# DLRM tower on one core: the first chunk by blocks of 8 examples, one plan for the layer-0 products, the gathers in two halves of a chunk, and transposes from the common rows

## The chip, the cores and the metric

One NeuronCore of a Trainium2 chip. The metric is the time of one execution on the device in microseconds (us), lower is better; it is taken over several executions and the median counts.

## What is computed

For each of 512 examples, 39 rows of 16 numbers are looked up in 39 tables (1,000 to 125,000 rows each) by `ids`. On them run three layers of a compressed interaction network, then a small MLP:

```python
def _cin_layer(X0, Xi, W, b):                 # X0: (512, 39, 16)
    Wr = W.reshape(H, F0_, Fi)                # H = 128
    return jnp.einsum('hjk,bjd,bkd->bhd', Wr, X0, Xi) + b[None, :, None]
...
for W, b in Ws:                               # three layers, Fi = 39, 128, 128
    Xi = _cin_layer(X0, Xi, W, b)
    res.append(Xi.sum(axis=2))
...
h = jnp.concatenate([z, dense_ctx], axis=1)   # (512, 384 + 16)
h = jnp.maximum(h @ W_top1 + b_top1, 0.0)     # 512
h = jnp.maximum(h @ W_top2 + b_top2, 0.0)     # 256
y = h @ W_top3                                # (512, 1)
```

## The kernel before

The 512 x 16 columns (example, dimension) are cut into 16 chunks (n = 0 to 15) of 32 examples, 512 columns; a chunk has 4 blocks (i = 0 to 3) of 8 examples, 128 columns. All engines run one program each, in an order written out by hand; semaphores that only count up tie them together. In the code "at (i, g)" names a place in a chunk: block i, and behind it the group of PE (g, 0 to 9), of ACT (a, 0 to 5), of DVE (d, 0 to 3) or of GpSimd (k, 0 to 3) after which a step comes.

- GpSimd (POOL) gathers the table rows of a chunk with 10 indirect DMAs (`gather`, each 128 rows of 64 B) into `emb`, and between them adds staged parts for layer 1 (`add`, L227, four a block). In chunk n it gathers chunk n + 3, the ten at the places `GATHER_AT`. Chunks 0, 1 and 2 are gathered at the head.
- SP's queue runs strictly in order, and a wait in it holds all that stands behind: `write_x` (from `emb` to the scratch `x_rows` in HBM, two halves of two DMAs), `load_xrow` (2 DMAs, the 39 rows for the transposes), `load_x` (from the scratch, shifted copies `shifted` and three copies of the 39 rows, `rows3`: 9 DMAs, 1.9 MB), and `copy_diag` (8 DMAs a pair of blocks, `xt` into the block-diagonal `diag` that layer 2's matmul reads). `body(n, u)` of SP is: write_x of the second half of chunk n + 2, load_xrow(n + 2), load_x(n + 2), copy_diag(n, pair 1), write_x of the first half of chunk n + 3, copy_diag(n + 1, pair 0).
- ACT copies the common rows to PSUM (`store_rows`, L685), DVE multiplies them with the shifted rows (`multiply_l0`, L395, seven tiles a chunk), PE contracts the products (`layer0`, L495, fp32, two passes a tile) into `quad_ps`. ACT and DVE split the result into `x1_hi` and `x1_lo`.
- Layer 1 on PE (`layer1`, L525): for each block ten groups of four fields, each three matmuls of 512 columns (hi x hi, hi x lo, lo x hi). ACT scales six groups a block by `xt` (L697), POOL adds them up, DVE scales and adds the other four (L424) and reduces all to `x2t` (L436).
- Layer 2's first step, `g_block` (L555), multiplies `x2t` of block i with `diag` of that block: at (i + 1, 9), so the g block of (n, 2) follows the last group of chunk n. `layer1` carries its wait, on the second of its three matmuls:

```python
    multiply(x1_hi, w1_hi, start=True)
    if g_of:
        pe.wait_ge(diag_copied[g_of[1] // 2], 16 * BLK_B * (g_of[0] + 1))
    ...
    multiply(x1_hi, w1_lo)
```

- `layer2` (L568) runs three times: in chunk 8, in chunk 15 and at the end, where the MLP follows.

Weights of layer 1 (2.5 MB, three parts) come over ACT's queue at the head; all three are split into hi and lo before layer 1 starts. Chunks 2 to 7 and 10 to 13 are loops in the code, the others are written out.

Of the kernel before, what the change touches and what calls it, by code (L numbers as in the profile page):

```python
# [7 lines left out]
F32 = mybir.dt.float32  # L8
# [14 lines left out]
CW = 512  # L23
# [38 lines left out]
BUFS = 3  # L62
# [11 lines left out]
LATE_HIGH_X1_AT, LATE_LOW_X1_AT = (3, 2), (3, 2)  # L74
NEXT_PRODUCTS_AT = {(2, 2): 0, (2, 3): 1, (3, 2): 2, (3, 3): 3}
PRODUCTS_AT = {(0, 2): 4, (0, 3): 5, (1, 0): 6}
FIRST_PRODUCTS_AT = {(1, 1): 0, (1, 2): 1, (1, 3): 2, (2, 0): 3, (2, 2): 4, (2, 3): 5, (3, 0): 6}
SECOND_PRODUCTS_AT = {(0, 0): 0, (0, 2): 1, (0, 3): 2, (1, 0): 3, (1, 2): 4, (1, 3): 5, (2, 0): 6}
# [23 lines left out]
assert all(len(fields_of(g)) == GF for g in A_GROUPS) and DUP == FPG * HALF_G and W2_FIRST > 0  # L102


def build(nc, ids, bases, tables, x_rows, w0a, w0b, w1, w2, biases, b1_row, ctx_in, wt1, wt1c, bt1, wt2, bt2, wt3,
          ident_in, mask_in, out):
    with ExitStack() as stack:
# [31 lines left out]
        rows3 = sb("rows3", [PK, 2, CW])  # L139
# [4 lines left out]
        xrow = sb("xrow", [FIELDS, CW])  # L144
# [26 lines left out]
        rows_picked = sem("rows_picked")  # L171
# [25 lines left out]

        def gathers_until(m):

            return 16 * HALF_G * (1 if isinstance(m, int) and m < BUFS else m - (BUFS - 2))  # L200

        @block.gpsimd
        def _(pool):
            def pick_rows(m, buf):
                ids_now = ids_sb[:, bass.ds(m, 1), :].rearrange("p a g -> p (a g)")
                nc.gpsimd.tensor_tensor(rows_now[:, buf, :], ids_now, bases_sb[:, :], ALU.add
                                        ).then_inc(rows_picked, 1)

                pool.wait_ge(rows_picked, m + 1)
                nc.gpsimd.tensor_tensor(passed[:, :], bases_sb[:, 0:1], bases_sb[:, 0:1], ALU.add)  # L210

            def gather(buf, g):
                parts = 128 if g < GATHERS - 1 else LAST_G
                nc.gpsimd.indirect_dma_start(  # L214
                    out=emb[0:parts, buf, g, :], out_offset=None, in_=tables[:, :],
                    in_offset=bass.IndirectOffsetOnAxis(ap=rows_now[0:parts, buf, g:g + 1], axis=0),
                ).then_inc(gathered[g // HALF_G][buf], 16)
# [12 lines left out]
            def body(n, gathering=True):  # L230
                for i in range(BLKS):
                    for k in range(ADDS):
                        add(n, i, k)
                        step = GATHER_AT.get((i, k))
                        if gathering and step is not None:
                            if step in (0, HALF_G):
                                half = step // HALF_G

                                pool.wait_ge(written[half], 32 * (n + 3))
                                if half == 0:  # L240

                                    pool.wait_ge(gathered[1][BUFS - 1], gathers_until(n + 2))
                                    pick_rows(n + 3, BUFS - 1)
                                else:
                                    nc.gpsimd.tensor_tensor(passed[:, :], bases_sb[:, 0:1], bases_sb[:, 0:1],
                                                            ALU.add)
                            gather(BUFS - 1, step)

            pool.wait_ge(ids_loaded, 32)
            for m in range(BUFS):  # L250
                pick_rows(m, m)
                for g in range(GATHERS):
                    gather(m, g)
            body(0)
            with pool.Fori(1, CHUNKS - 3) as n:
                body(n)
            with pool.Fori(CHUNKS - 3, CHUNKS) as n:
                body(n, gathering=False)

        @block.sync  # L260
        def _(sp):
# [3 lines left out]
            def write_x(m, half, buf):  # L265
                there = value(gathers_until(m))
# [13 lines left out]
            def load_x(m, u):  # L280
                all_written = value(32 * (m + 1))
# [544 lines left out]
```

## Time and profile before

| what | value |
|---|---|
| median of 3 runs | 710.0 us (707.98 to 715.27) |
| the profiled execution, own time | 709.59 us |
| its span in the profile | 707.8 us |
| PE busy | 650.3 us, 92% |
| DVE, POOL, ACT busy | 506.6, 490.1, 479.0 us |
| mean granted clock of PE | 0.995 |

The span runs from the first to the last instruction; the own time has 1.8 us around it. A busy share of 92% does not say that PE works at its peak: its matmuls are pipelined and their ends modelled. Idle time before an instruction stands in brackets behind it with what ended it.

### The profile page before, as it was taken

Reading aid. Unit: us, or ns where it says so; the run is one execution under the profiler, and the core shown is the slowest. Engines: PE = TensorE matmul, PEld = TensorE weight load, DVE = VectorE, ACT = ScalarE, POOL = GpSimd, SP = SyncE. Lnnn points to the kernel's source line nnn. Section 1 sums busy time; section 2 is a strip of 40 time slices with the busy share of each in tenths; the row PEclk is TensorE's granted clock in tenths of the full one; section 3 lists DMA queues with packets and bytes.
Section 4 is the critical chain, followed back from the end, with each engine's and each line's share of the span. In section 5 each row is a group of like instructions: output and inputs, shape, how many; then the busy total and the mean of one; then the engine's idle time right before and its main releaser. Section 6 shows DMA issues by size and latency. Waiting matters only on the chain.

```text
span 707.8 us, 12139 instructions
## 1 busy us (share of the span) xinstructions
PE 650.3 (92%) x2622; PEld 469.6 (66%) x2622; DVE 506.6 (72%) x1177; ACT 479.0 (68%) x1730; POOL 490.1 (69%) x465
## 2 busy tenths in 40 slices
PE   0097889999999999999999999999989999999998
PEld 0055567777677777777787677777767777778763
DVE  2345588979697979798853797979777979784810
ACT  2145577878687878686935778787767868784802
POOL 5767478878787878888854787878786845453700
PEclk9999999999999999999999999999999999999999
DMA  8660425151515151515140041322323040002000
GB/s 208 126 131 12 110 38 114 40 109 27 120 29 118 28 119 28 120 28 118 29 109 13 10 113 17 81 49 67 63 61 67 7 116 4 2 4 81 0 1 0
DMA packets 65776, 44.51 MB, mean 63 GB/s; under 512 B 49563, under 2 KB 58062, under 8 KB 63860
## 3 DMA queue, kind: packets, MB, share of 16 engines
q1 hardware_dynamic: 54610, 39.35, 25.1%
q0 software_dynamic: 5120, 1.29, 2.1%
q10 hardware_dynamic: 6002, 3.39, 1.8%
q8 instruction: 14, 0.23, 0.1%
q14 instruction: 30, 0.25, 0.1%
HBM read 40.78 MB, written 1.94 MB: 60 GB/s over the span
## 4 chain that ended last, share of the span: by engine, by line
PE 71%; DVE 8%; DMA 6%; issue 4%; POOL 4%; SPq 3%; ACT 3%; DVEq 0%; ACTq 0%; POOLq 0%
PE a_ps L525 28%; PE d_ps L525 18%; PE quad_ps L495 11%; DVE x2t L436 6%; PE quad_ps L568 5%; PE g_ps L555 5%; POOL emb L214 3%; ACT parts L697 2%; DMA rows<-x_rows 2%; DVE parts L424 2%; DMA x_rows<-emb 2%; DMA emb<-tables_dram,rows_now 1%; SPq L320 1%; PE a_ps L654 1%; POOL parts L227 1%
## 5 line engine op out<-in xcount | busy, mean ns | idle before, releaser
L697 ACT ACTIVATE parts<-a_ps,xt 128x128 f32<-128x128 f32 x1536 | 426.5, 397 | 117.9 <-PE a_ps L525 113.6
L227 POOL TENSOR_TENSOR parts<-parts 128x512 f32<-128x512 f32 x256 | 327.3, 1294 | 143.8 <-ACT parts L697 141.4
L424 DVE SCALAR_TENSOR_TENSOR parts<-d_ps,xt,parts 128x128 f32<-128x128 f32 x832 | 236.0, 343 | 90.0 <-PE d_ps L525 82.4
L525 PE MATMUL a_ps<-w_hi,x_hi 128*128 128x512 f32 x384 | 178.0, 464 | 1.8 <-ACT x_hi L668 0.9
L214 POOL DMA_INDIRECT emb<-tables_dram,rows_now x160 | 154.0, 962 | 29.1 <-issue 20.6
L436 DVE TENSOR_REDUCE x2t<-parts 128x128 f32<-128x1280 f32 x64 | 157.4, 2459 | 4.2 <-POOL parts L227 4.2
L525 PE MATMUL a_ps<-w_hi,x_lo 128*128 128x512 f32 x384 | 153.6, 400 | 2.9 <-DVE z L405 2.5
L525 PE MATMUL a_ps<-w_lo,x_hi 128*128 128x512 f32 x384 | 152.3, 397 | 1.2 <-ACT xt L678 1.2
L495 PE MATMUL quad_ps<-products,w_sb 117*128 117x512 f32 (+1 forms) x224 | 116.6, 606 | 13.0 <-DVE products L395 13.0
L525 PE MATMUL d_ps<-w_hi,x_hi 128*128 128x512 f32 (+1 forms) x256 | 124.3, 486 | 0.0
L525 PE MATMUL d_ps<-w_lo,x_hi 128*128 128x512 f32 (+1 forms) x256 | 97.6, 381 | 2.5 <-DMA diag<-xt 2.5
L525 PE MATMUL d_ps<-w_hi,x_lo 128*128 128x512 f32 (+1 forms) x256 | 97.8, 382 | 0.0
L525 PEld LDWEIGHTS a_ps<-w_hi,x_hi 128*128 128x128 f32 x384 | 72.5, 189 | 31.4 <-issue 7.5
L525 PEld LDWEIGHTS a_ps<-w_lo,x_hi 128*128 128x128 f32 x384 | 72.7, 189 | 25.2 <-issue 5.7
L525 PEld LDWEIGHTS a_ps<-w_hi,x_lo 128*128 128x128 f32 x384 | 72.4, 189 | 24.4 <-DVE z L405 6.5
L395 DVE TENSOR_TENSOR products<-shifted,rows_ps 117x512 f32<-117x512 f32 x112 | 75.5, 678 | 11.6 <-ACT rows_ps L685 11.6
L525 PEld LDWEIGHTS d_ps<-w_lo,x_hi 128*128 128x128 f32 x256 | 48.5, 189 | 26.0 <-issue 15.1
L525 PEld LDWEIGHTS d_ps<-w_hi,x_hi 128*128 128x128 f32 x256 | 48.1, 188 | 23.8 <-issue 7.7
L495 PEld LDWEIGHTS quad_ps<-products,w_sb 117*128 117x128 f32 (+1 forms) x224 | 42.8, 194 | 27.0 <-issue 10.7
L525 PEld LDWEIGHTS d_ps<-w_hi,x_lo 128*128 128x128 f32 x256 | 48.2, 188 | 8.6
L555 PE MATMUL g_ps<-diag,x2t 128*128 128x320 f32 x128 | 47.8, 455 | 6.4 <-DVE x2t L436 6.4
L424 DVE SCALAR_TENSOR_TENSOR parts<-d_ps,xt,b_rows 128x128 f32<-128x128 f32 x64 | 22.4, 350 | 42.9 <-PE d_ps L525 39.7
(52 smaller groups left out, 278.1 us busy)
## 6 DMA issues: line engine op xcount, KB each, us to landing
shifted<-x_rows SPq DMA_DIRECT2D x48, 312.0 KB
shifted<-x_rows SPq DMA_DIRECT2D x48, 234.0 KB
diag<-xt SPq DMA_DIRECT2D x256, 4.9 KB
rows<-x_rows SPq DMA_DIRECT2D x48, 78.0 KB
emb<-tables_dram,rows_now POOLq DMA_INDIRECT x160, 2.4
g_sb<-w_dram ACTq DMA_DIRECT2D x3, 832.0 KB, 10.4
w_sb<-w_dram SPq DMA_DIRECT2D x7, 320.0 KB, 3.0
x_rows<-emb SPq DMA_DIRECT2D x32, 40.0 KB
```

Source lines behind the costliest of these rows:

```text
L214: nc.gpsimd.indirect_dma_start(out=emb[0:parts, buf, g, :], out_offset=None, in_=tables[:, :], in_offset=bass.IndirectOffsetOnAxis(ap=rows ...
L227: nc.gpsimd.tensor_tensor(parts[:, i % 2, now:now + GF, :], parts[:, i % 2, now:now + GF, :], parts[:, i % 2, more:more + GF, :], ALU.add) ...
L320: sp.dma_start(diag[rows, blks, b, 0:FIELDS], xt[rows, u, blks, :]).then_inc(diag_copied[pair], 16)
L395: nc.vector.tensor_tensor(products[0:PK, t, :], shifted[0:PK, t, :], rows_ps[0:PK, :], ALU.mult).then_inc(products_ready, 1)
L424: nc.vector.scalar_tensor_tensor(now, d_ps[d % D_RING][:, H * at:H * (at + 1)], xt[:, u, i, j:j + 1], before, ALU.mult, ALU.add).then_inc( ...
L436: nc.vector.tensor_reduce(x2t[:, i % 2, :], parts[:, i % 2, 0:PARTS_LEFT, :].rearrange("p k h -> p h k"), AX_X, ALU.add).then_inc(x2t_read ...
L495: nc.tensor.matmul(quad_ps[:, :], w0_sb[0:rows, t, :], products[0:rows, t, :], start=(t == 0), stop=(t == QT - 1)).then_inc(products_used, 1)
L525: return nc.tensor.matmul(bank[:, 0:H * len(fields)], x[:, u, 128 * i:128 * (i + 1)], w[:, fields[0]:fields[-1] + 1, :].rearrange("p j h - ...
L555: nc.tensor.matmul(g_ps[:, 0:(FIELDS + 1) * BLK_B], x2t[:, i % 2, :], diag[:, i, :, :].rearrange("p b j -> p (b j)"), start=True, stop=Tru ...
L568: mm = nc.tensor.matmul(z3_ps[:, 0:(c1 - c0) * CB], w2_sb[:, j, :], g_sb[:, j, c0 * CB - base:c1 * CB - base], start=(j == 0), stop=(j == ...
L654: mm = nc.tensor.matmul(a_ps[1 + mt][:, :], wt2_sb[:, kt, 128 * mt:128 * (mt + 1)], h1[:, kt, :], start=(kt == 0), stop=(kt == N1 // 128 - 1))
L697: last = nc.scalar.activation(parts[:, i % 2, 2 + GF * a + at, :], a_ps[(NA * i + a) % A_RING][:, H * at:H * (at + 1)], ACT.Copy, scale=xt ...
```

## The change

1. Chunk 0 goes by blocks of 8 examples. Its rows are gathered by 12 indirect DMAs (3 a block, 16 fields each), written to a scratch of its own (`x_first`, 5 DMAs a block) and loaded from there (6 DMAs a block); products (`multiply_first`, one instruction a block), layer 0 (`layer0_first`, 7 matmuls of 128 columns), the split, the transposes (to `rows_ps`) and `diag` (`diag_first`, on DVE from a mask, in place of DMAs) follow by block. Layer 1 starts when block 0 is there. The third part of the weights is split after block 0's x1.
2. One plan of the products for all chunks: chunk n makes the seven products of chunk n + 1 in its first half (`PRODUCTS_AT`); before, four of chunk n + 2 came in the second half. Chunk 1 has a later plan.
3. In chunk n GpSimd gathers the second half of chunk n + 2 at the first five places of `GATHER_AT` and the first half of chunk n + 3 at the last five. Before, it gathered all of chunk n + 3.
4. `xrow` and `load_xrow` are gone: the transposes read `rows3`, which has one buffer now in place of two, and `load_x(m)` waits for the transposes of chunk m - 1.
5. The copy of the common rows moves from ACT's (1, 4) to (3, 4), the transposes from PE's (0, 5) to (0, 6), and the g block of (n - 1, 3) from (0, 9) to (1, 1), except in chunks 8 and 15. The w2 loads go in 7 pieces in place of 8.

The diff, cut to its core:

```diff
+FPG0 = 128 // BLK_B
+GATHERS0 = -(-FIELDS // FPG0)
-BUFS = 3
+BUFS = 2
...
-TRANSPOSE_AT, FIRST_TRANSPOSE_AT = (0, 5), (1, 5)
+TRANSPOSE_AT, LATE_TRANSPOSE_AT = (0, 6), (0, 9)
-G_AT, STORE_G_AT = 9, 5
+G_AT, STORE_G_AT = {(1, 9): 0, (2, 9): 1, (3, 9): 2}, {(1, 5): 0, (2, 5): 1, (3, 5): 2}
+LAST_G_AT, STORE_LAST_G_AT = (1, 1), (1, 0)
...
-NEXT_PRODUCTS_AT = {(2, 2): 0, (2, 3): 1, (3, 2): 2, (3, 3): 3}
-PRODUCTS_AT = {(0, 2): 4, (0, 3): 5, (1, 0): 6}
+PRODUCTS_AT = {(0, 0): (0,), (0, 2): (1,), (0, 3): (2,), (1, 0): (3,), (1, 2): (4,), (1, 3): (5,), (2, 0): (6,)}
...
-ROWS_AT, FIRST_ROWS_AT, SECOND_ROWS_AT = {(1, 4): 2}, {(1, 0): 1, (3, 4): 2}, {(2, 2): 2}
-GATHER_AT = {(0, 1): 0, (0, 3): 1, (1, 1): 2, (1, 2): 3, (1, 3): 4, (2, 1): 5, (2, 3): 6, (3, 1): 7, (3, 2): 8, (3, 3): 9}
+ROWS_AT, LATE_ROWS_AT = (3, 4), (0, 5)
+FIRST_TRANSPOSE_AT, FIRST_STORE_XT_AT = {(0, 4): 1, (1, 4): 2, (1, 9): 3}, {(0, 2): 1, (1, 2): 2, (2, 0): 3}
+FIRST_L0_AT, FIRST_HIGH_X1_AT = 5, 3
+FIRST_G_AT, FIRST_STORE_G_AT = {(2, 3): 0, (3, 2): 1, (3, 9): 2}, {(2, 2): 0, (3, 1): 1, (3, 5): 2}
+SECOND_TRANSPOSE_AT, SECOND_STORE_XT_AT, SECOND_ROWS_AT = (3, 0), (3, 0), (2, 5)
+SECOND_L0_AT = {(3, 3): 0, (3, 4): 1, (3, 5): 2, (3, 6): 3, (3, 7): 4, (3, 8): 5, (3, 9): 6}
+SECOND_HIGH_X1_AT = (3, 5)
+GATHER_AT = ((0, 1), (0, 3), (1, 1), (1, 2), (1, 3), (2, 1), (2, 3), (3, 1), (3, 2), (3, 3))
+FIRST_GATHER_AT = 3 * ((0, 3),) + 3 * ((1, 3),) + 4 * ((2, 3),) + ((3, 1), (3, 2), (3, 3))
+FIRST_GATHERS = 10
+MORE_GATHERS = (13, 12)
...
         @block.gpsimd
+            def steady(n, u, last=False):
+                order = [(n + 2, u, g) for g in range(HALF_G, GATHERS)]
+                if not last:
+                    order += [(n + 3, 1 - u, g) for g in range(HALF_G)]
+                return {at: [step] for at, step in zip(GATHER_AT, order)}
...
+            for i in range(BLKS):
+                for g in range(GATHERS0):
+                    gather_first(i, g)
+            first = [(m, m % 2, g) for m in range(1, 5) for g in range(GATHERS)]
+            for m, u, g in first[0:FIRST_GATHERS]:
+                gather(m, u, g)
...
         @block.sync
+            def write_first(i):
+                sp.wait_ge(first_gathered[i], 16 * GATHERS0)
...
+                for g in range(GATHERS0):
+                    write(FPG0 * g, g, 128 if g < GATHERS0 - 1 else LAST_G0)
+                write(FIELDS, 0, 128)
+                write(FIELDS + FPG0, 1, BLK_B * (DUP - FPG0))
+            def load_first(i):
+                sp.wait_ge(first_written[i], 16 * (GATHERS0 + 2))
+                cols = slice(128 * i, 128 * (i + 1))
+                for s in reversed(range(SPT)):
+                    rows = slice(FIELDS * s, FIELDS * (s + 1))
+                    src = bass.AP(x_first.tensor, i * X_ROWS * 128, [[128, FIELDS], [1, 128]])
+                    sp.dma_start(rows3[rows, cols], src).then_inc(first_loaded[i], 16)
+                    src = bass.AP(x_first.tensor, (i * X_ROWS + s * QT) * 128, [[128, FIELDS], [128, QT], [1, 128]])
+                    sp.dma_start(shifted[rows, :, cols], src).then_inc(first_loaded[i], 16)
...
+            for i in range(BLKS):
+                write_first(i)
+                load_first(i)
+            write_x(1, 0)
+            write_x(1, 1)
+            load_x(1)
+            write_x(2, 0)
+            copy_diag(1, 1, 0)
+            write_x(2, 1)
+            load_x(2)
...
+            copy_diag(1, 1, 1)
+            write_x(3, 0)
+            write_x(3, 1)
+            load_x(3)
+            copy_diag(2, 0, 0)
+            load_w2(0, W2_FIRST)
+            write_x(4, 0)
             def body(n, u, loading=True, writing=True, last=False):
                 if loading:
-                    write_x(n + 2, 1, 2)
-                    load_xrow(n + 2)
-                    load_x(n + 2, u)
+                    write_x(n + 2, 1)
+                    load_x(n + 2)
                 copy_diag(n, u, 1)
                 if last:
                     return
                 if writing:
-                    write_x(n + 3, 0, 2)
+                    write_x(n + 3, 0)
                 copy_diag(n + 1, 1 - u, 0)
...
         @block.vector
+            def multiply_first(i):
+                dve.wait_ge(first_loaded[i], 32 * SPT)
+                cols = slice(128 * i, 128 * (i + 1))
+                rows = rows3[:, cols].unsqueeze(1).to_broadcast([PK, QT, 128])
+                nc.vector.tensor_tensor(products[0:PK, :, cols], shifted[0:PK, :, cols], rows, ALU.mult
+                                        ).then_inc(first_products, 1)
...
+            def diag_first(i):
+                dve.wait_ge(xt_ready, i + 1)
+                x = rows_ps[:, FIELDS * i:FIELDS * (i + 1)].unsqueeze(1).to_broadcast([128, BLK_B, FIELDS])
+                at = mask[:, :].unsqueeze(2).to_broadcast([128, BLK_B, FIELDS])
+                nc.vector.tensor_tensor(diag[:, i, :, 0:FIELDS], x, at, ALU.mult).then_inc(first_diag, 1)
...
         @block.tensor
+            def layer0_first(i):
+                pe.wait_ge(first_products, i + 1)
+                cols = slice(128 * i, 128 * (i + 1))
+                for t in range(QT):
+                    rows = PK if t < QT - 1 else QT_LAST
+                    mm = nc.tensor.matmul(quad_ps[:, cols], w0_sb[0:rows, t, :], products[0:rows, t, cols],
+                                          start=(t == 0), stop=(t == QT - 1))
+                mm.then_inc(first_summed, 1)
...
                 multiply(x1_hi, w1_hi, start=True)
-                if g_of:
-                    pe.wait_ge(diag_copied[g_of[1] // 2], 16 * BLK_B * (g_of[0] + 1))
+                if is_zero(q) and g in W1_PART_AT:
+                    pe.wait_ge(w1_lo_ready, W1_PART_AT[g] + 1)
+                elif g_of:
+                    if is_zero(g_of[0]):
+                        pe.wait_ge(first_diag, g_of[1] + 1)
+                    else:
+                        pe.wait_ge(diag_copied[g_of[1] // 2], 16 * BLK_B * g_of[0])
...
         @block.scalar
+            split_w1(0)
+            split_w1(1)
+            store_xt_first(0)
             act.wait_ge(bias_ready, 1)
-            high_x1(0, 0)
+            high_first(0)
+            split_w1(2)
             act.wait_ge(w1_lo_ready, 3)
```

## Rows read from the trace of the kernel before

**Rows 1.** Page part 1: busy time, share, instructions; then part 4, the chain by engine.

```profile
PE 650.3 (92%) x2622; PEld 469.6 (66%) x2622; DVE 506.6 (72%) x1177; ACT 479.0 (68%) x1730; POOL 490.1 (69%) x465
...
PE 71%; DVE 8%; DMA 6%; issue 4%; POOL 4%; SPq 3%; ACT 3%; DVEq 0%; ACTq 0%; POOLq 0%
```

**Rows 2.** Timeline of DVE, the sum at a chunk's head: start, duration; chunks 0, 1, 5, 6.

```profile
47.37 0.68 DVE L405 TENSOR_REDUCE z<-quad_ps 128x32 f32<-128x512 f32 x1
...
95.45 0.68 DVE L405 TENSOR_REDUCE z<-quad_ps 128x32 f32<-128x512 f32 x1
...
244.19 0.68 DVE L405 TENSOR_REDUCE z<-quad_ps 128x512 f32 x1
...
280.98 0.67 DVE L405 TENSOR_REDUCE z<-quad_ps 128x512 f32 x1
```

**Rows 3.** Timeline of all engines, 0 to 45 us: start, duration, engine, operation, [idle before].

```profile
7.29 0.95 POOL L214 DMA_INDIRECT emb<-tables_dram,rows_now  x1 [0.31 <-issue]
...
10.10 1.09 DVE L460 TENSOR_TENSOR w_sb<-w_sb,g_sb 117x896 f32<-117x896 f32 x1 [10.10 <-DMA g_sb<-w0b_dram]
...
16.98 4.05 SPq L271 DMA_DIRECT2D x_rows<-emb  x4
...
22.15 0.64 SPq L309 DMA_DIRECT2D xrow<-x_rows  x2
...
33.35 0.59 ACT L685 COPY rows_ps<-rows 117x512 f32<-117x512 f32 x1 [12.90 <-DMA rows<-x_rows]
...
34.81 8.65 PE L495 MATMUL quad_ps<-products,w_sb 117*128 117x512 f32 x14 [7.25 <-DVE products L395]
...
44.40 0.47 PE L525 MATMUL a_ps<-w_hi,x_hi 128*128 128x512 f32 x1 [0.93 <-ACT x_hi L668]
```

**Rows 4.** Timeline of SP's queue, chunk 5.

```profile
247.75 1.02 SPq L271 DMA_DIRECT2D x_rows<-emb  x2
249.95 0.67 SPq L309 DMA_DIRECT2D xrow<-x_rows  x2
251.06 0.31 SPq L295 DMA_DIRECT2D shifted<-x_rows  x1
...
255.42 5.17 SPq L320 DMA_DIRECT2D diag<-xt  x8
```

**Rows 5.** Timeline of POOL, chunk 5.

```profile
245.26 0.92 POOL L214 DMA_INDIRECT emb<-tables_dram,rows_now  x1 [0.16 <-issue]
...
260.19 0.96 POOL L214 DMA_INDIRECT emb<-tables_dram,rows_now  x1 [0.16 <-issue]
262.64 1.29 POOL L227 TENSOR_TENSOR parts<-parts 128x512 f32<-128x512 f32 x1 [1.49 <-ACT parts L697]
264.08 0.96 POOL L214 DMA_INDIRECT emb<-tables_dram,rows_now  x1 [0.15 <-issue]
```

**Rows 6.** Timeline of ACT, chunk 5: the copy of the common rows.

```profile
260.82 0.59 ACT L685 COPY rows_ps<-rows 117x512 f32<-117x512 f32 x1 [2.32 <-DMA rows<-x_rows]
```

**Rows 7.** Timeline of PE, second matmul of chunk 5's last group.

```profile
276.19 0.34 PE L525 MATMUL d_ps<-w_lo,x_hi 128*128 128x384 f32 x1
```

**Rows 8.** DMA view, 245 to 285 us, one digit each us: tenths busy of the 16 engines.

```profile
DMA  0002103787988788730000350100010650001010
```

**Rows 9.** Timeline of PE: three idle stretches, and what follows the last.

```profile
62.77 1.34 PE L495 MATMUL quad_ps<-products,w_sb 117*128 117x512 f32 x2 [2.75 <-DVE products L395]
...
91.82 0.45 PE L525 MATMUL d_ps<-w_lo,x_hi 128*128 128x384 f32 x1 [2.49 <-DMA diag<-xt]
...
523.12 0.49 PE L525 MATMUL a_ps<-w_hi,x_lo 128*128 128x512 f32 x1 [2.48 <-DVE z L405]
...
524.57 0.63 PE L525 MATMUL d_ps<-w_hi,x_lo 128*128 128x512 f32 x1
```

**Rows 10.** Windows: busy us by engine, then granted clock (1.00 is full), DMA share.

```profile
60.00:70.00 10.00, 7.25 (x22) 4.95 (x21) 7.04 (x16) 3.21 (x12) 8.69 (x8) 0.83 0.05 6
90.00:100.00 10.00, 8.18 (x37) 6.49 (x38) 8.03 (x19) 6.88 (x27) 8.00 (x8) 1.00 0.19 21
```

More of the change, by code:

```diff
@@ L94, with is_late @@
 NDF = len(D_FIELDS)
+W1_PART_AT = {0: 0, 3: 1, 6: 2}
+def is_late(n):
+    return isinstance(n, int) and n == LATE
 def is_zero(count):
@@ L210, in pick_rows, with gather @@
+                pool.wait_ge(rows_picked, m)
                 nc.gpsimd.tensor_tensor(passed[:, :], bases_sb[:, 0:1], bases_sb[:, 0:1], ALU.add)
-            def gather(buf, g):
-                parts = 128 if g < GATHERS - 1 else LAST_G
+            def gather(m, u, g):
+                parts, half, buf = 128 if g < GATHERS - 1 else LAST_G, g // HALF_G, buf_of(m)
+                if g in (0, HALF_G):
+                    if not (isinstance(m, int) and m < 3):
+                        pool.wait_ge(written[half], 32 * (m - 1))
+                    if half == 0:
+                        pick_rows(m, u)
+                    elif not (isinstance(m, int) and m < 3):
+                        nc.gpsimd.tensor_tensor(passed[:, :], bases_sb[:, 0:1], bases_sb[:, 0:1], ALU.add)
@@ L233, in body @@
                         add(n, i, k)
[L234 to L258, printed above, removed]
+                        for m, u, g in gathers_at.get((i, k), ()):
+                            gather(m, u, g)
[4 more added lines that the diff above has]
+                return {at: [step] for at, step in zip(GATHER_AT, order)}
@@ new lines, in _ @@
+            for m, u, g in first[0:FIRST_GATHERS]:
+                gather(m, u, g)
+            done = FIRST_GATHERS
+            for n, count in enumerate(MORE_GATHERS):
+                gathers_at = {}
+                for at, step in zip(MORE_GATHER_AT if n else FIRST_GATHER_AT, first[done:done + count]):
+                    gathers_at.setdefault(at, []).append(step)
+                body(n, gathers_at)
+                done += count
+            with pool.Fori(1, CHUNKS // 2 - 2) as h:
+                for u in range(2):
+                    body(2 * h + u, steady(2 * h + u, u))
@@ L260, in _ @@
+            body(CHUNKS - 4, steady(CHUNKS - 4, 0))
+            body(CHUNKS - 3, steady(CHUNKS - 3, 1, last=True))
+            with pool.Fori(CHUNKS - 2, CHUNKS) as n:
+                body(n, {})
         @block.sync
@@ L443, in body @@
                         add_group(n, u, i, d)
-                        if d == REDUCE_AT and not (first and i == 0):
+                        if d == REDUCE_AT:
                             reduce_parts(n - (i == 0), (i - 1) % BLKS)
@@ L475, in _ @@
-            ahead = (1, PRODUCTS_AT), (2, NEXT_PRODUCTS_AT)
-            body(0, 0, [(1, FIRST_PRODUCTS_AT)], first=True)
-            body(1, 1, [(1, SECOND_PRODUCTS_AT), (2, NEXT_PRODUCTS_AT)])
+            dve.wait_ge(w0_loaded, 32)
+            nc.vector.tensor_tensor(w0_sb[:, :, :], w0_sb[:, :, :], w0b_sb, ALU.add).then_inc(w0_ready, 1)
+            split_w1(0)
+            multiply_first(0)
+            split_w1(1)
+            low_first(0)
+            split_w1(2)
+            diag_first(0)
@@ new lines, in _ @@
+            for i in range(BLKS):
+                add_group(0, 0, i, 0)
+                if i == 0:
+                    multiply_first(1)
+                elif i == 3:
+                    multiply_l0(1, 2)
+                    multiply_l0(1, 3)
+                add_group(0, 0, i, 1)
+                if i > 0:
+                    reduce_parts(0, i - 1)
+                if i < BLKS - 1:
+                    low_first(i + 1)
+                    diag_first(i + 1)
+                else:
+                    multiply_l0(1, 4)
+                    multiply_l0(1, 5)
+                if i == 2:
+                    sum_x1(0)
+                add_group(0, 0, i, 2)
+                if i < 2:
+                    multiply_first(i + 2)
+                else:
+                    multiply_l0(1, 0 if i == 2 else 6)
+                add_group(0, 0, i, 3)
+                if i == 2:
+                    multiply_l0(1, 1)
```

399 lines of the change are left out of this document (245 added, 154 removed).

## The prediction

> **What bounds the kernel now.** I read the page first: PE is busy 92% of the span and 71% of the chain that ended last is PE's, with no other engine over 8% [rows 1]. So time can only be won where PE stands still, and anything that makes PE stand still inside a chunk is paid in full. Next the sums at the chunk heads, which date the chunks [rows 2]: between chunks 5 and 6 lie 36.8 us, between 0 and 1 48.1 us. The first sum came 3.0 us after PE's first layer-1 matmul (44.40, [rows 3]), so chunk 1 began at about 92.4. Then the timeline of the head [rows 3]: PE begins layer 1 at 44.4, behind gathers (one each 1.26 us on POOL), writes from 16.98, loads from 22.15, common rows that land for ACT at 33.35, and 14 passes of layer 0 in 8.65 us. There are 44 us of head and 11 us of stalls in chunk 0; in the other chunks PE has almost none. Last I read one steady chunk, 5, queue by queue [rows 4 to 7], because parts 3 and 5 of the change move work there.
>
> **The head (parts 1 and 4).** Block 0 needs three gathers: the third starts at about 8.0 (7.29 is the second of before) and is issued by 9. Before, the first five gathers were issued by 12.0 and SP wrote at 16.98, 5 us later, while the weights filled the DMA engines; I take the same 5 us less a little, 13.5. Five writes at about 0.5 us and their landing: 18. Six load issues of 0.4 us end at 20.5. The full chunk's load took from 22.15 to 33.35; block 0's is a quarter of it, 0.47 MB, in packets of 512 B: I take 3.5 us of landing, so 24 (bounds 22.5 and 29, nothing less and as long as before). One product instruction of 896 columns costs 1.1 us by the add over 117x896 [rows 3]; seven matmuls of 128 columns in 14 passes I take at 2.5 us (a quarter of 8.65 us is the floor, 8.65 the ceiling); the split to x1_hi 0.3. Layer 1 starts at 28.5 in place of 44.4.
>
> Chunk 0 then holds the PE work of a steady chunk, 36.8, and three more layer0_first of 2.2 us, 43.4. To that come 1.7 us in block 0, where ACT and DVE first split the third part of the weights and PE runs out of free banks, about 1.5 us at the end, where PE waits for x1 of chunk 1 behind ACT's last copies, and 1 us for chunk 1's common rows: 47.6. SP needs about 6.7 us a block (7 writes and copies, landing, 6 loads) and PE over 9, so blocks 1 to 3 are there in time. On DVE, diag_first and low_first cost under 1 us a block and hide beside PE. Chunk 1 starts at 76 in place of 92.4: -16.4 us. Bounds: -10 (block loads as slow as before) and -20 (no stall in chunk 0).
>
> **The products plan (part 2).** The same seven products, none added. In block 0 DVE now has 13 adds, a reduce, the sum and three products, some 9 us beside 7.5 of PE, but d_ps lets it lag and it catches up in block 1. Zero on the path; if the cover goes, under 1 us a chunk.
>
> **GpSimd half a chunk later in effect (part 3).** This I follow in chunk 5's own times. In SP's queue the order is write_x(n + 2, second half), load_x(n + 2), copy_diag(n, pair 1). Before, the gathers behind the first of these ended with the chunk before, the write went at 247.75 and the diag copies at 255.42 [rows 4]; PE wants them at its wait on the second matmul of the last group, 276.19 [rows 7], 15 us after they were issued. Now the last gather that write_x waits for stands at (1, 3). In the trace that place is the gather at 264.08, held up by ACT [rows 5], which stood 2.32 us for the common rows [rows 6]; with that copy moved, POOL runs on without a gap: gather at 260.19 for 0.96, add of 1.29, next gather at 262.6 [rows 5]. From there:
> - gather to write: 245.26 to 247.75, 2.5 us [rows 4, 5]: 265.1;
> - write to landed, 247.75 to 249.95, 2.2 [rows 4]: 267.3, where load_x starts at once, xrow's 1.1 us being gone;
> - first load to first diag copy, 251.06 to 255.42, 4.4, and 5.2 for eight diag copies [rows 4]: issued by 276.9, already later than 276.2;
> - landing: they stand in the same queue behind 1.9 MB of load. The digits show the engines busy from 251 to about 263, 12.2 us from the first load [rows 8], and nothing after: last diag bytes at about 279.6, 280.0 with the signal.
>
> So PE stands still for about 3.8 us a chunk, and I take 3.9 with its restart. Lower bound: the copies land 1.2 us after their issue, as the two writes did (248.77 to 249.95, [rows 4]), at 278.1: 1.9 us. Upper bound 5. Everything in this chain hangs on the place (1, 3) of the same chunk, so a longer chunk does not relieve the next. It holds for chunks 2 to 13, the twelve in which SP loads two chunks ahead: 12 x 3.9 = +46.8 us. The same kind of wait already stands once in the trace: at 91.82 PE was idle 2.49 us for diag copies stuck behind chunk 1's load [rows 9].
>
> The Trainium skill, DMA: Bandwidth & Descriptors, section Anatomy of one DMA, gives about 2.0 us of fixed cost from issue to signal. By it the last diag copy, issued from 276.3, is there at 278.3, the wait is 2.1 us, and the whole comes to some 738 us; the digits speak for the longer one, since the copies queue behind the load.
>
> **The clock.** After PE had been idle 2.75 us (to 62.77) the granted clock averaged 0.83 in 60 to 70, 1.7 us of full speed lost [rows 9, 10]; after 2.48 us (to 523.12) matmuls went from 0.40 to 0.63 us [rows 9]; after 2.49 us (to 91.82) nothing happened, clock 1.00 [rows 9, 10]. A wait of 3.9 us is longer than all three. I take one fall to 1.2 GHz a chunk: 12 x 1.7 = +20.4 us. Bounds 0 and twice that. The Trainium skill, TensorE: Matmul & The Clock Gate, section HAM oscillation, tells of a kernel whose every tile waits on a DMA and starts at the lower level; the trace agrees in two of three cases.
>
> **The rest.** The moved g block keeps its work; the copy of the common rows at (3, 4) would find them landed at about 277 (260.82 came 9.8 us after the first load, from 267.4), 1 us late for ACT, within PE's stall. The end of the kernel is the same: 0.
>
> **The sum** against the profiled execution, whose own time (709.59) is at the median (710.0): span 707.8 - 16.4 + 46.8 + 20.4 = 758.6, and 1.8 around it: 760 us. A change under 1% (7 us) can't be told from none here.
>
> **The rivals.**
> - A, the forecast: the wait at (3, 9) in twelve chunks, with the lower clock behind it. Per chunk 2.5 to 5 us and a fall of 1.7: 740 to 777. Chance 0.66.
> - B, the wait is there but short, and the clock holds: 707.8 - 16.4 + 1.8 + 12 x 1.9 = 716, up to 740 with 3.9. For it: one of three idle stretches of this length left the clock alone, and the engines may drain sooner without xrow's 78 KB. Against it: the queue order. Chance 0.17.
> - C, faster: diag copies land before (3, 9). It decides at the 13.6 us that the chunk leaves from the gather (262.6) to the wait of PE (276.2); I count 17.4. If POOL had its gather out 1.8 us sooner (no backlog of its own), the writes landed in 1.5 and the copies were not held by the load, it would just fit. Then only the head counts: 707.8 - 16.4 + 1.8 = 693, 686 to 703 by the head's bounds. For it: the head's gain is the surest part, and every item of the chain could shrink a little. Against it: issues on SP alone (4.4 + 5.2) are fixed. Chance 0.12.
> - D, both the wait of A and a head that does not do what it says: the block loads in 512 B packets take as long as the full one, layer 1 starts at 37 and the lower clock comes twice: 777 to 795. Chance 0.05.
>
> The likeliest is A, 760. The range 716 to 777 holds A and B. Faster by over 1% (under 703) is C: 0.12; within 1% the low end of B and the high end of C: 0.04; slower 0.84.
>
> **What the profile after would show.** Sums at chunk heads 42.5 us apart in chunks 2 to 13 (36.8 in chunk 1 and 14) if A holds, 36.8 everywhere under C, 39 to 41 under B. PE's idle time before the second matmul of each chunk's last group, put down to the diag copies, 3.9 us, and a granted clock near 0.96 over a steady chunk. On SP, write_x in mid-chunk with the diag copies behind the load. First layer-1 matmul at 28.5, chunk 1's sum at 79. I would be wrong most simply if the gather at (1, 3) came out earlier than 21.5 us after the chunk's start, or if the diag copies overtook the load in the engines.

## The result and the profile after

The changed kernel took 790.7 us, the median of 4 runs (788.93 to 794.28), beside 710.8 us of the kernel before on the same chip (707.98 to 715.27): a ratio of 1.1115, interval 1.1068 to 1.1161. The forecast was 760 with a range of 716 to 777. It went slower as expected, by the mechanism expected, and further than the range allowed.

Parts 1 and 4 of the page after, as in [rows 1], and the row of part 5 that names the cause:

```profile
PE 678.1 (86%) x2664; PEld 495.4 (63%) x2664; DVE 512.3 (65%) x1180; ACT 485.8 (62%) x1735; POOL 492.9 (63%) x467
...
PE 43%; DMA 18%; SPq 13%; issue 10%; POOL 8%; ACT 4%; DVE 4%; POOLq 0%; ACTq 0%; DVEq 0%
...
L686 PE MATMUL d_ps<-w_lo,x_hi 128*128 128x512 f32 (+1 forms) x256 | 104.7, 409 | 69.4 <-DMA diag<-xt 69.4
```

PE fell from 92% to 86% of the span, and from 71% to 43% of the chain that ended last; DMA and SP's queue took its place. One group of instructions carries nearly all of PE's new idle time: the second matmul of a chunk's last group, released by the diag copies.

The view of waits of PE after (us in total, times, longest):

```profile
PE d_ps L686 <- DMA diag<-xt: 69.4, 12, 7.4
PE rows_ps L641 <- DMA shifted<-x_first: 24.1, 1, 24.1
PE a_ps L686 <- ACT parts L906: 5.6, 2, 5.4
PE a_ps L686 <- DMA rows<-x_rows: 2.7, 1, 2.7
```

Twelve waits on the diag copies, the number forecast, but 5.8 us each. The third row was not forecast at all.

The sums at the chunk heads, as in [rows 2], here of chunks 0, 1, 4 and 5 on DVE's timeline:

```profile
59.62 0.68 DVE L516 TENSOR_REDUCE z<-quad_ps 128x32 f32<-128x512 f32 x1
...
82.08 0.68 DVE L516 TENSOR_REDUCE z<-quad_ps 128x32 f32<-128x512 f32 x1
...
216.79 0.68 DVE L516 TENSOR_REDUCE z<-quad_ps 128x512 f32 x1
...
260.83 0.68 DVE L516 TENSOR_REDUCE z<-quad_ps 128x512 f32 x1
```

Chunk 1 begins 13.4 us sooner than before (95.45 to 82.08); a steady chunk takes 44.0 us and not 36.8. The windows from the head of chunk 2 to that of chunk 14, first after, then before, split what the twelve chunks lost (us, then busy us of each engine, granted clock, DMA share, GB/s):

```profile
119.12:677.33 558.21, 483.77 (x1832) 356.40 (x1833) 374.78 (x878) 358.69 (x1297) 363.98 (x344) 0.92 0.27 54
```

```profile
132.74:597.59 464.85, 456.39 (x1831) 335.34 (x1830) 372.75 (x877) 349.54 (x1286) 358.33 (x337) 1.00 0.30 63
```

The stretch is 93.4 us longer. PE is idle for 74.4 us in it, where it had been idle for 8.5: +66.0. And it is busy 27.4 us longer with the same matmuls, at a granted clock of 0.92 in place of 1.00. The whole span is then: head -13.4, chunk 1 -0.3, chunks 2 to 13 +93.4, end +0.9, in all +80.6 (707.8 to 788.4).

One chunk, queue by queue, as in [rows 4 to 7]; the chain of work through the middle of chunk 4 (start, us, what):

```profile
235.84 2.24 DMA emb<-tables_dram,rows_now
...
238.27 0.39 SPq L367
...
238.85 1.40 DMA x_rows<-emb
...
240.68 0.36 SPq L396
...
249.71 5.27 DMA diag<-xt
```

Gather, write and first load stand 4.8 us apart, as forecast (4.7). The rest is on SP's and PE's timelines:

```profile
240.68 0.36 SPq L396 DMA_DIRECT2D shifted<-x_rows  x1
...
245.21 5.09 SPq L409 DMA_DIRECT2D diag<-xt  x8
```

```profile
249.23 0.34 PE L686 MATMUL d_ps<-w_hi,x_hi 128*128 128x384 f32 x1
255.02 0.69 PE L686 MATMUL d_ps<-w_lo,x_hi 128*128 128x384 f32 x1 [5.46 <-DMA diag<-xt]
```

The last copy was issued at 249.71 and released PE 5.3 us later. What the DMA engines did meanwhile is in the DMA view from 250 to 256 us, one digit each 0.15 us:

```profile
DMA  5969988595785851200000000000031000000000
```

The busy stretch ends at about 252.6, 11.9 us after the load's first issue; the forecast had 12.2 [rows 8]. The two digits at 254.4 to 254.6 look like the last diag bytes, but they are a gather's. The DMA view counts packets by queue: q1 is SP's, q0 GpSimd's. Its windows 252.9 to 254.0, 253.2 to 254.2 and 254.2 to 254.8 us:

```profile
q1 hardware_dynamic: 22, 0.00, 2.0%
...
DMA packets 0, 0.00 MB, mean 0 GB/s; under 512 B 0, under 2 KB 0, under 8 KB 0
...
q0 software_dynamic: 32, 0.01, 13.6%
```

The last packets of SP's queue start before 253.2 (the last diag packet at 253.12 in the trace), 12.4 us after the load's first issue, where the forecast had 12.3. After that SP's queue moves nothing, and yet PE is released only at 255.02: 1.9 us pass between the last diag packet and the signal. The forecast had 0.4.

PE's clock after the wait, in windows (PE's busy time comes first, the granted clock third from the end):

```profile
250.00:255.00 5.00, 0.00 (x0) 0.00 (x0) 1.23 (x5) 1.66 (x5) 4.67 (x5) 0.83 0.38 83
255.00:256.00 1.00, 0.98 (x3) 0.98 (x4) 0.00 (x0) 0.00 (x0) 0.84 (x2) 0.50 0.00 0
256.00:258.00 2.00, 2.00 (x6) 1.42 (x5) 0.87 (x3) 0.49 (x2) 0.15 (x1) 0.50 0.05 4
258.00:260.00 2.00, 2.00 (x6) 1.52 (x6) 0.21 (x1) 1.14 (x4) 0.00 (x0) 0.50 0.40 41
260.00:262.00 2.00, 2.00 (x10) 1.64 (x9) 2.00 (x6) 1.34 (x6) 0.00 (x0) 0.97 0.05 8
```

The level drops to 0.50, 1.2 GHz, while PE stands, and stays there for 5 us of work: six matmuls in 2 us in place of ten.

### The profile page after: what moved, and what is told of

Read it like the earlier page. It is cut to its first block, busy times and chain, and to the rows that moved or that the text cites. A ratio compares the mean times of both kernels' runs of the same rounds, so it can differ in the third digit from the quotient of the medians.

```text
span 788.4 us, 12165 instructions
## 1 busy us (share of the span) xinstructions
PE 678.1 (86%) x2664; PEld 495.4 (63%) x2664; DVE 512.3 (65%) x1180; ACT 485.8 (62%) x1735; POOL 492.9 (63%) x467
## 4 chain that ended last, share of the span: by engine, by line
PE 43%; DMA 18%; SPq 13%; issue 10%; POOL 8%; ACT 4%; DVE 4%; POOLq 0%; ACTq 0%; DVEq 0%
PE a_ps L686 17%; PE d_ps L686 11%; DMA diag<-xt 8%; SPq L409 6%; PE quad_ps L637 5%; POOL parts L291 5%; ACT parts L906 4%; DMA emb<-tables_dram,rows_now 4%; SPq L396 3%; PE g_ps L727 3%; DMA x_rows<-emb 2%; POOL emb L271 2%; PE quad_ps L740 2%; DVE x2t L549 2%; DMA rows<-x_rows 2%
## 5 line engine op out<-in xcount | busy, mean ns | idle before, releaser
L686 PE MATMUL a_ps<-w_hi,x_hi 128*128 128x512 f32 x384 | 190.0, 495 | 7.4 <-ACT parts L906 5.6
L686 PE MATMUL d_ps<-w_lo,x_hi 128*128 128x512 f32 (+1 forms) x256 | 104.7, 409 | 69.4 <-DMA diag<-xt 69.4
L271 POOL DMA_INDIRECT emb<-tables_dram,rows_now x150 | 145.5, 970 | 26.6 <-issue 17.8
L686 PE MATMUL a_ps<-w_lo,x_hi 128*128 128x512 f32 x384 | 157.6, 410 | 2.7 <-DMA rows<-x_rows 2.7
L637 PE MATMUL quad_ps<-products,w_sb 117*128 117x512 f32 (+1 forms) x210 | 107.3, 591 | 0.0
L686 PE MATMUL d_ps<-w_hi,x_lo 128*128 128x512 f32 (+1 forms) x256 | 102.6, 401 | 0.0
L686 PEld LDWEIGHTS a_ps<-w_hi,x_hi 128*128 128x128 f32 x384 | 76.3, 199 | 35.9 <-issue 10.7
L915 ACT COPY g_sb<-g_ps 128x312 f32 (+1 forms) x64 | 27.0, 422 | 103.8 <-PE g_ps L727 103.0
L485 DVE TENSOR_TENSOR products<-shifted,rows_ps 117x512 f32<-117x512 f32 x105 | 70.8, 676 | 5.8 <-ACT rows_ps L894 5.8
L727 PE MATMUL g_ps<-diag,x2t 128*128 128x320 f32 x128 | 52.4, 495 | 1.7 <-DVE x2t L549 1.7
```

Source lines behind the costliest of these rows:

```text
L271: nc.gpsimd.indirect_dma_start(out=emb[0:parts, buf, g, :], out_offset=None, in_=tables[:, :], in_offset=bass.IndirectOffsetOnAxis(ap=rows ...
L485: nc.vector.tensor_tensor(products[0:PK, t, :], shifted[0:PK, t, :], rows_ps[0:PK, :], ALU.mult).then_inc(products_ready, 1)
L637: nc.tensor.matmul(quad_ps[:, :], w0_sb[0:rows, t, :], products[0:rows, t, :], start=(t == 0), stop=(t == QT - 1)).then_inc(products_used, 1)
L686: return nc.tensor.matmul(bank[:, 0:H * len(fields)], x[:, u, 128 * i:128 * (i + 1)], w[:, fields[0]:fields[-1] + 1, :].rearrange("p j h - ...
L727: nc.tensor.matmul(g_ps[:, 0:(FIELDS + 1) * BLK_B], x2t[:, i % 2, :], diag[:, i, :, :].rearrange("p b j -> p (b j)"), start=True, stop=Tru ...
L915: nc.scalar.copy(g_sb[:, :, bass.ds(col - half * HB, BLK_B)], g[:, 0:FIELDS, :])
```

## The experiments

Two theories went into them. The first: SP's order is at fault, so that the diag copies stand behind a gather, a write and 1.9 MB of load which the change moved ahead of them, and the lower clock follows from PE standing still. The rivals: the new load itself is too late or too slow in its new place, whatever stands behind it; or the new product plan and the gathers cost time of their own. Each edit is against the changed kernel unless it says otherwise. Ratios are to the kernel before, timed beside each.

**e1: the diag copies first.**

```diff
 def body(n, u, loading=True, writing=True, last=False):
+    copy_diag(n, u, 1)
     if loading:
         write_x(n + 2, 1)
         load_x(n + 2)
-    copy_diag(n, u, 1)
```

> The kernel after, with SP's copy_diag(n, pair 1) moved ahead of write_x(n + 2) and load_x(n + 2). Theory (the diag copies stand in SP's queue behind a load that waits for late gathers): the wait of 69.4 us on diag goes, and with it the lower clock behind it (some 25 us over twelve chunks); chunk heads 36.8 to 37.5 us apart, 690 to 700 us in all, faster than before (710). Rival (the plan itself is too tight: seven products in the first half, common rows copied at (3, 4) from rows that land late): another wait takes its place, on ACT's parts or the rows, chunks of 39 to 41 us, 720 to 750 us.

Measured: 712.6 us, ratio 1.0008 (0.9974 to 1.0042). Steady chunks are 36.8 us again and the granted clock of the run rose from 0.944 to 0.983: one line of order on one queue gives back 78 us. The chain of cause is shown. But the size expected (690 to 700) was missed, by two further waits. PE's waits:

```profile
PE a_ps L686 <- ACT parts L906: 8.7, 3, 5.8
PE quad_ps L740 <- DMA w_sb<-w_dram: 7.2, 1, 7.2
```

The first lies in chunk 2 (5.8 of the 8.7 us), where the common rows of a later chunk land too late for ACT. It stands in the changed kernel too, as 5.4 us ahead of the first diag wait. The second is new and comes once, at layer 2, where the diag waits had covered it; SP's and PE's timelines show it:

```profile
354.60 5.08 SPq L409 DMA_DIRECT2D diag<-xt  x8
359.90 0.40 SPq L431 DMA_DIRECT2D w_sb<-w_dram  x1
```

```profile
363.21 3.33 PE L740 MATMUL quad_ps<-g_sb,w_sb 128*128 128x256 f32 x7 [7.23 <-DMA w_sb<-w_dram]
```

PE had run out at 356.0 for weights which SP issued only at 359.90, behind eight diag copies.

**e2: the mid-chunk gathers one place earlier.**

```diff
-GATHER_AT = ((0, 1), (0, 3), (1, 1), (1, 2), (1, 3), ...
+GATHER_AT = ((0, 1), (0, 3), (1, 0), (1, 1), (1, 2), ...
```

> The kernel after, with the last gather that write_x(n + 2) waits for one place earlier, at (1, 2) in place of (1, 3), 2.4 us on POOL. Theory: the wait on diag falls by the same 2.4 us a chunk, from 5.5 to 3.1, chunks of 42 us, 755 to 762 us, or some 20 us less if the clock holds over a wait of 3 us. Rival (the wait is set by the DMA engines' load, not by when POOL's last gather goes): no change, 785 to 790 us.

Measured: 768.0 us, ratio 1.0787 (1.0735 to 1.0839), slower than expected. The twelve waits on the diag copies shrank to 43.0 us, 3.6 each.

**e3: the same gathers as early as the chunk allows.**

```diff
-GATHER_AT = ((0, 1), (0, 3), (1, 1), (1, 2), (1, 3), ...
+GATHER_AT = ((0, 0), (0, 1), (0, 2), (0, 3), (1, 0), ...
```

> The kernel after, with the five gathers of chunk n + 2 at (0, 0), (0, 1), (0, 2), (0, 3), (1, 0), so that the last leaves POOL some 6 to 7 us earlier. Theory: no wait on diag and no fall of the clock, chunks of 37 us, 692 to 705 us, with SP's order unchanged. Rival (POOL has no room: two more gathers in block 0 make its adds late, and the reduce, and PE's g blocks): a wait on x2t or parts of 2 us a chunk, 715 to 730 us.

Measured: 714.5 us, ratio 1.0066 (1.0036 to 1.0097), above the 692 to 705 expected: 7.7 us of diag waits are left, and beside them 6.8 us on ACT's parts and 6.4 us on the weights of layer 2. With SP's order as in the changed kernel, POOL's places alone bring nearly all of it back. The dose follows: last mid-chunk gather at (1, 3), (1, 2), (1, 0) gives diag waits of 69.4, 43.0, 7.7 us and a ratio of 1.1115, 1.0787, 1.0066.

**e4: the diag copies between write and load.**

```diff
     write_x(n + 2, 1)
-    load_x(n + 2)
 copy_diag(n, u, 1)
+if loading:
+    load_x(n + 2)
```

> The kernel after, with copy_diag(n, pair 1) between write_x(n + 2) and load_x(n + 2). Theory: the copies are issued 4.5 us earlier and are not behind the load's bytes, they land about 10.3 us after the gather, PE wants them after 13.6: no wait on diag. But the load goes 5.2 us later, the common rows reach ACT 5 us late at (3, 4), and PE waits 3 to 4 us a chunk for ACT's parts: chunks of 41 to 42 us, 745 to 765 us. Rival (only the diag copies matter): 690 to 700 us.

Measured: 774.6 us, ratio 1.088 (1.0819 to 1.094), above the 745 to 765 expected. No diag wait was left, and the time fell by only 16 us. What took its place, in PE's waits, and the ACT instruction behind it in one of the chunks:

```profile
PE a_ps L687 <- ACT parts L907: 46.1, 14, 5.5
```

```profile
251.53 0.59 ACT L895 COPY rows_ps<-rows 117x512 f32<-117x512 f32 x1 [4.76 <-DMA rows<-x_rows]
```

The load now starts 5 us later, and ACT stands at the copy of the common rows with the relu of PE's banks queued behind it. So the rival is half right: the load has no room to be late either. Of the three orders only e1's, where the diag copies go while the gathers are still under way, makes neither wait for the other.

**e5: a small load in front.** The second half of each load moves 32 of its 512 columns; tiles 4 to 6 are therefore mostly old data.

```diff
-sp.dma_start(shifted[rows, t0:t1, :], src)
+w = 32 if half == 1 else CW
...
+sp.dma_start(shifted[rows, t0:t1, 0:w], src)
```

> The kernel after, with the second half of each load_x (shifted tiles 4 to 6) cut to 32 of 512 columns, so that part of the products is made of old data: 0.66 MB less a chunk, issues in number and order the same. If the diag copies are held by the bytes in front of them in the DMA engines, as the prediction had it, the wait falls from 5.5 to 2.5 to 3 us, chunks of 41 to 42 us, about 750 us. If issue on SP and a fixed time from the last byte to the signal make it, it stays at 5 or more, 780 to 790 us.

Measured: 747.0 us in a single run, beside 709.1 of the kernel before. The waits, `34.1, 12, 4.4` in the view, are 2.8 us each in place of 5.8, with SP's issues unchanged in number and place. So of each wait 3 us are the bytes in front, and the rest is the chain of issues up to the last copy and that copy's own landing. In one chunk of this run the last copy, issued at 243.87, had its last packet at 245.29 and released PE at 246.63: 1.4 and 1.3 us, in place of 3.4 and 1.9 in the changed kernel.

**e6: the wait filled with matmuls.** 26 matmuls of 384 columns are added ahead of the wait at (3, 9) in the looped chunks; their result is overwritten.

```diff
+if g_of and (i, g) == (3, 9) and not isinstance(n, int):
+    for _ in range(26):
+        multiply(x1_hi, w1_hi, start=True, stop=True)
 multiply(x1_hi, w1_hi, start=True)
```

> The kernel after, with 26 extra matmuls of 384 columns (4.6 us, written over by the group that follows) ahead of the wait on diag at (3, 9) in the ten chunks that are in loops (2 to 7, 10 to 13); the wait of 5.5 us stays but PE is busy in most of it. Theory (the lower clock behind each wait costs some 2 us a chunk and comes from PE's idleness): chunk heads 42.3 us apart in place of 44.4, granted clock back near 0.99, 765 to 772 us. Rival (the 2 us beyond the wait have another cause, late parts or rows): no change, 786 to 792 us.

Measured: 768.5 us, ratio 1.084 (1.0779 to 1.09), some 20 us less than the changed kernel although PE does more. PE's timeline at the place:

```profile
244.02 4.93 PE L686 MATMUL d_ps<-w_hi,x_hi 128*128 128x384 f32 x27
249.52 0.45 PE L686 MATMUL d_ps<-w_lo,x_hi 128*128 128x384 f32 x1 [0.57 <-DMA diag<-xt]
```

and the window from 200 to 300 us, where the changed kernel has a granted clock of 0.92:

```profile
200.00:300.00 100.00, 97.67 (x420) 75.44 (x418) 73.21 (x169) 69.26 (x252) 71.88 (x69) 1.00 0.30 62
```

The copies land as late as before; only the stillness is gone, and the clock with it stays at 1.00. That is the clock's share by itself in ten of the twelve chunks: 20 us.

**e7: e1, and chunk 1's gathers earlier.**

```diff
-MORE_GATHER_AT = ((0, 1), (0, 3), (1, 1), (1, 3), (2, 0), (2, 1), ...
+MORE_GATHER_AT = ((0, 0), (0, 1), (0, 2), (0, 3), (1, 1), (1, 2), ...
```

> e1 (diag copies first) with chunk 1's gathers at earlier places (the seven of chunk 3 all by (1, 3)), so that chunk 3's common rows land before ACT wants them at (3, 4) of chunk 1. Theory: PE's wait of 5.8 us on ACT's parts in chunk 2 goes: 705 to 708 us. Rival (POOL too full in chunk 1, its adds late): no gain, 712.

Measured: 706.3 us, ratio 0.9956 (0.9926 to 0.9986). Chunk 2 went from 44.6 to 36.7 us: its stall came from chunk 1's gathers.

**e8: e7, and the weights of layer 2 ahead of the chunk's other transfers.**

```diff
 for u in range(2):
-    body(2 * h + u, u)
     load_w2(...)
+    body(2 * h + u, u)
```

> e7 with each load of w2 ahead of SP's body in the loop in place of behind it, so that the last is not behind the diag copies of chunk 8. Theory: PE's wait of 7.2 us on w2 before layer 2 in chunk 8 goes too: 697 to 701 us, 1.5 to 2% under the kernel before. Rival (w2's bytes held the engines anyway): 704 to 708.

Measured: 697.1 us, ratio 0.9827 (0.9788 to 0.9867). With all three faults away the steady chunks take 36.8 us, the same as before the change, and chunk 1 starts 11.9 us sooner. So the whole worth of the change is the head; the products plan and the new places of the gathers neither give nor cost anything once nothing waits behind them.

**e9: e8, and the product of block 3 sooner.** In chunk 0 the product of block 3 took 4.3 us on DVE, beside four adds of POOL in a row, and delayed chunk 1's load. It is moved from the third group of block 1 to the first.

```diff
-if i == 0:
-    multiply_first(1)
+if i < 2:
+    multiply_first(2 * i + 1)
 ...
-if i < 2:
-    multiply_first(i + 2)
-else:
+if i == 0:
+    multiply_first(2)
+elif i > 1:
     multiply_l0(1, 0 if i == 2 else 6)
```

> e8 with chunk 0's multiply_first(3) on DVE moved from behind group 2 of block 1 to behind its group 0, where POOL gathers and does not add. In the kernel after this one product took 4.47 us in place of 1.08, exactly as long as POOL's four adds ran (47.77 to 52.78), and load_x(1) waited for it until 53.9. Theory (an instruction of DVE with two SBUF operands stands still beside POOL's adds): it takes 1.1 us at about 44.5, load_x(1) starts at 50 to 51 when the last transpose is done, PE's wait of 2.8 us for the rows of chunk 1 shrinks below 1, chunk 1's sum at 80.5 to 82, 693 to 696 us. Rival (that product is slow by its shape or its source): it stays at 4 us, 697.

The product on DVE's timeline, in e8 and then in e9:

```profile
49.34 4.30 DVE L492 TENSOR_TENSOR products<-shifted,rows 117x896 f32<-117x896 f32 x1
```

```profile
44.65 1.62 DVE L492 TENSOR_TENSOR products<-shifted,rows 117x896 f32<-117x896 f32 x1
```

Measured: 691.7 us, ratio 0.9675 (0.9637 to 0.9714), the fastest version of the study. PE's wait of 2.8 us for the common rows of chunk 1 is gone, and the head of chunk 1 moved from 83.59 to 79.12 us; 1.5 us of that are not the edit's, since the first load of this execution landed at 22.8 us and that of e8 at 24.3. So the edit is worth about 3 us; the ratios of e8 and e9 lie further apart because they come from two chips, on which the kernel before took 709.1 and 713.8.

**e10: late diag copies in the kernel before.** The edit is to the kernel before: eight diag copies go behind a write, which waits for a late gather, but behind no load.

```diff
+if writing and not last:
+    write_x(n + 3, 0, 2)
 copy_diag(n, u, 1)
 if last:
     return
-if writing:
-    write_x(n + 3, 0, 2)
```

> The kernel before with one swap in SP's body: write_x(n + 3, first half) ahead of copy_diag(n, pair 1), so that the diag copies go some 11 us later in the chunk (about 26 us in, landed by 33.5), behind a wait for gathers but not behind a load. Theory (what hurts is the load in front of them, to past 35 us): PE waits little or nothing for diag, 708 to 713 us, the same as before. Rival (any diag copy that waits for POOL's gathers costs): a wait of 1 to 3 us a chunk and the lower clock, 725 to 760 us.

Measured: 714.4 beside 713.8 us, ratio 0.9982 (0.9942 to 1.0023). SP's timeline:

```profile
272.34 1.01 SPq L271 DMA_DIRECT2D x_rows<-emb  x2
273.59 10.41 SPq L320 DMA_DIRECT2D diag<-xt  x16
```

No wait on them came in the steady chunks. The profiled execution has a span of 721.0 us, longer than the median, so only its order and its waits are read here. The first eight copies follow each other by 0.65 us, so the last of them was issued at about 278.1; the matmul that needs them ran at 282.17 without a wait. The last signal on their semaphore stands in the trace at 279.82: they landed in 1.7 us with no load in front, and in 5.3 in the changed kernel behind one. So a place behind a late gather costs nothing by itself; it is the load, with the time it needs to be issued and moved, that makes the copies too late.

## Why the prediction was right in kind and wrong in size

The expected terms and what the trace and the runs gave, in us:

| term | forecast | measured | why |
|---|---|---|---|
| head, to the start of chunk 1 | -16.4 | -13.4 | layer 1 slow at first, a product of 4.5 us |
| diag waits, chunks 2 to 13 | +46.8 (12 x 3.9) | +69.4 (12 x 5.8) | mostly the time from the last bytes to the signal |
| other idle time of PE there | 0 | -3.4 | 5.0 left (most of it in chunk 2) where before had 8.5 |
| lower clock there | +20.4 (12 x 1.7) | +27.4 (12 x 2.3) | the stretch at 1.2 GHz |
| chunk 1 and the end | 0 | +0.6 | |
| span | 758.6 | 788.4 | |

**The step that failed** is the last one in the count of the diag copies, "last diag bytes at about 279.6, 280.0 with the signal": it gives 0.4 us from the bytes to the signal. Everything ahead of it held: the place (1, 3) as the last gather, PE's own time from that gather to its wait (13.6 forecast, 13.7 measured, from 235.84 to 249.56), gather to load 4.8 (4.7), first load to the last diag packet 12.4 (12.3). Then came 1.9 us to the release of PE, 14.3 us after the first load. In eleven of the twelve chunks this step takes 1.85 to 2.33 us; in the last, copies for the next chunk follow so closely that the packets can't be told apart. It alone makes 1.5 of the 1.7 us by which the wait of chunk 4 was longer than forecast. Over the twelve chunks the mean wait is 5.8 us.

In the steady chunks of before no one waited for these copies, so none of [rows 1 to 10] priced their landing, but the trace had it: in chunk 5 the last diag packet starts at 263.58 and the last signal on their semaphore stands at 265.51. The upper bound of 5 should have been an open one, say the busy stretch and then a landing of 2.2 us as writes have [rows 4], which comes to a wait of 5.5. The wait at 91.82 [rows 9], which the prediction set beside this one, was no guide to its size. The load in front of it was chunk 2's and not chunk 1's, and its last packets were over by 88.7; the last copy, issued at 89.82, landed in 1.95 us.

The Trainium skill, DMA: Bandwidth & Descriptors, section Anatomy of one DMA, gives about 2.0 us of fixed cost for a transfer issued on GpSimd, most of it between the last byte and the signal; these copies stand on SP's queue. Taken as the whole landing it gave a wait of 2.1 us and was far off; as an estimate, set behind the forecast's 12.2 us of load, it comes to 14.2 us from the first load, and the trace has 14.3.

**The clock** was right in sign and in number, one fall a chunk. The size came from a fall after 2.75 us of idle time, with 1.7 us lost [rows 9, 10]; here the wait is 5.5 us, and 1.2 GHz holds for 5.2 us of work (255.0 to 260.2). Matmuls of 512 columns follow each other every 0.43 us in it and not every 0.235, which loses 2.3 us, and PE's busy time says the same (27.4 / 12). e6 shows that it is the stillness that costs it. The Trainium skill, TensorE: Matmul & The Clock Gate, section HAM oscillation, describes tiles that each wait for a DMA and begin at the lower level; this kernel now does so in all twelve chunks, where the matmul behind the wait takes 0.69 us each time.

**The head** came as forecast up to layer 1: the first load lands at 24.07 (24), layer 1 starts at 29.09 (28.5). Then three things were not priced. PE's first matmuls take 0.63 us until 34.3, so the stretch from 29.1 costs 2.3 us more. The product of block 3 took 4.47 us. And with it the load of chunk 1 came late, for which PE stood 2.7 us where 1 was forecast. Three rows of after, of the timelines of PE and DVE:

```profile
24.07 0.30 PE L641 MATMUL rows_ps<-ident,rows 39*128 39x39 f32 x1 [24.07 <-DMA shifted<-x_first]
...
29.09 0.77 PE L686 MATMUL a_ps<-w_hi,x_hi 128*128 128x512 f32 x1 [0.57 <-issue]
```

```profile
49.27 4.47 DVE L492 TENSOR_TENSOR products<-shifted,rows 117x896 f32<-117x896 f32 x1
```

**The common rows** were said to be 1 us late for ACT within PE's stall. In the steady chunks this is right: ACT stood 0.3 us for them in chunk 4, at 250.19. In chunk 2 it is not. Chunk 1's gathers stand at other places, and ACT stood 6.95 us and PE 5.4; I had looked at the steady chunk alone. e7 settles it.

**The products plan** at zero is right: e8's steady chunks equal those before.

**The rivals.** C, faster, needed 13.6 us from the gather to the last copy's signal; it took 19.2. That point was rightly named as the one that decides: e3 takes the gathers earlier and e1 takes the copies out of the chain, and with e1 the wait goes, with e3 nearly so. What C expected to be left, 686 to 703, is e8's 697 only after the two further faults were mended. B and D did not occur: the clock never held, and the small block loads were as fast as forecast.

What stays open: why the signal of copies behind a load comes 1.9 us after their last packet. In the same execution the next eight copies, with no load in front, had their last packet at 264.85 and their last signal at 265.20, 0.4 us later. e5 shows that the gap shrinks with the bytes in front (1.3 us), but no run here varied the number or the size of the copies.

## What to carry to other kernels

Before moving a write-then-load pair up in a queue, list what stands behind it in that queue and for whom, then put the small transfers that an engine needs soon ahead of the pair: here one line's order was worth 78 us of 790. Small copies behind a large load are to be priced as the load's busy stretch and then a landing of their own (1.9 us here), not as its last bytes. Before a digit of the DMA view is given to a transfer, look at which queue moved it. A wait that a change adds can cover another, as the diag waits did one of 7.2 us here, and others stand beside it; after mending the first, read the waits again, and read the first and last iterations with their own schedules as well as the steady one.

## What the runs showed of the hardware

Eight copies of 4.9 KB on SP's queue land 1.7 to 1.8 us after the issue of the last with no load in front (e10 278.1 to 279.82; changed kernel 263.43 to 265.20), and 5.3 us after it behind 1.9 MB of load (249.71 to 254.98). Of the 3.5 us more, 2.0 lie ahead of their last packet and 1.5 behind it.

DVE's product of two operands in SBUF (117x896) takes 1.08 us alone and 4.30 to 4.47 us when POOL runs four adds in a row beside it. POOL's timeline of the changed kernel, beside DVE's row at 49.27 above:

```profile
47.77 5.01 POOL L291 TENSOR_TENSOR parts<-parts 128x512 f32<-128x512 f32 x4
```

The product with its second operand in PSUM took 0.68 us in the mean over 105 of them, with POOL busy beside many. DVE's product ended at 53.7, after POOL's train had ended at 52.8. The Trainium skill, SBUF — State Buffer, section SBUF: two separate sides, says that a DVE operation with two SBUF inputs and a GpSimd operation that reads SBUF hold a shared pair of ports as an exclusive lock; the rows agree, and moving the product away from the train (e9) brought it to 1.62 us. In e9 two adds still ran when it began (POOL 42.07 for 3.25, DVE 44.65). The product ends 0.96, 0.97 and 0.95 us after the last add of the train in the changed kernel, e8 and e9: it stands until the train is over and then takes nearly its own time.

PE's first matmuls of layer 1 take 0.63 us for 5.2 us of work, as after a wait in mid-kernel, but the granted clock of that window (29 to 34 us) reads 1.00, whereas after the waits it reads 0.50. A start of the kernel at 1.00 can therefore not be trusted to mean full speed; durations show it.
